# A two-layer block of phase mixer and ternary feed-forward: the context's inverse deviation goes through a DRAM row, and its statistics follow the first hidden unit

## The chip, the cores and the metric

One Trainium2 chip, one of its cores. The metric is the device time of the kernel in microseconds (us), lower is better. Before the change the median of 3 runs is 1516.18 us (1516.14 to 1516.83). One further execution was profiled.

## The reference, cut to what matters

x is 16 sequences of 1024 rows of 256 float32. One layer of each kind is applied:

```python
# mixer, on xn = layernorm(x), with a residual from xn and one from x
omega = xn @ W_omega.T + b_omega
phi = cumsum(omega * exp(log_scale) / sqrt(position), axis=1)
cm_real, cm_imag = xn * cos(phi), xn * sin(phi)
mem_real, mem_imag = cumsum(cm_real) / position, cumsum(cm_imag) / position
ret_real = mem_real * cos(phi) + mem_imag * sin(phi)
ret_imag = mem_imag * cos(phi) - mem_real * sin(phi)
context = concatenate([cm_real, cm_imag, ret_real, ret_imag])      # 1024 wide
h = layernorm(context) * ln_gamma + ln_beta
h = gelu(h @ W1.T + b1)                                            # 512 hidden units
x = x + xn + (h @ W2.T + b2)
# feed-forward with weights quantized to -1, 0, 1, on layernorm(x)
x = x + relu(layernorm(x) @ Wq1.T + b1f) @ Wq2.T + b2f             # 1024 hidden units
```

## The kernel before

The rows are cut into 32 chunks of 512 rows (`CH`), two per sequence. A chunk lives on chip with its features on the 128 partitions and its 512 rows along the free dimension. Matmuls run in float16 with high and low parts (`hi`, `lo`) of activations and weights, so a hidden unit block of the mixer (`hidden`, L967 to L984) takes 24 matmuls of 512 columns.

The kernel is written as one program per engine, each a fixed list of work, tied together by semaphores (`need`, `need_sum`, `need_block` wait for the counter of a named step and chunk). `run` calls `step(s)` for s = -1 to 31 on each engine. In step s, four chunks are in hand: `now` = s (its feed-forward), `nxt` = s+1 (its mixer's two products), `ahead` = s+2 (phases, sums and context), `far` = s+3 (first normalization and the product with W_omega). The order inside a step is written by hand for each engine. Three special stretches stand apart from the 29 full steps (s = 0 to 28): the preparation of weights with step -1, then step 29 which has no `far`, and the last two steps (`last_mixer` and the end of the feed-forward).

TensorE in a full step: `hidden` 0 and 1, `context_stats`, `hidden` 2, `spread`, `hidden` 3, then the feed-forward in a skewed order: `ffn_in` 0 to 3, `ffn_out` 0, `ffn_in` 4, `ffn_out` 1, `ffn_in` 5, `omega`, `ffn_out` 2, `ffn_in` 6, `ffn_out` 3, `ffn_in` 7, `ffn_out` 4, `mixer_out`, `ffn_out` 5 to 7.

The context's layer normalization is folded behind the W1 product. `context_stats` (L952, L958) sums the context and its squares over the features by matmuls with a column of ones, so mean and square sum come out with rows on partitions. `context_variance` on VectorE (L1363 to L1375) makes the variance, `inverse_std_context` on GpSimd (L514) raises it to the power -1/2, into `crs` (128 x 4). But the product with W1 has features on partitions and rows along the free dimension, so the 512 inverse deviations are needed as one row repeated on all 128 partitions (`rb`). `spread` (L965) makes it by four TensorE transposes of a broadcast column of `crs` into PSUM, and `spread_out` on ScalarE (L675) copies it to `rb`. `scale_hidden` on VectorE (L1382) multiplies each of the four hidden blocks in PSUM by `rb`; ScalarE then applies `gelu` (L679) and makes the high part (`gelu_hi`, L685), VectorE the low part (`gelu_lo`, L1387), and `mixer_out` (L1038) reads both.

The feed-forward's hidden block m goes `ffn_in` (L1004) on TensorE, `relu` (L713) and `relu_hi` (L722) on ScalarE, `relu_lo` (L1426) on VectorE, `ffn_out` (L1017) on TensorE. Its input is turned from rows to features by DMA transposes that SyncE issues (L445), after `second_hi` (L695, ScalarE) and `second_lo` (L1418, VectorE).

GpSimd also issues the accumulating DMAs: `base_bias` (L497), `x1_bias` (L501), `output_sum` (L505), `retrieve` (L490, L493) and `square_sums` (L543).

The ternary feed-forward weights are made on chip too: `signs` on VectorE (L1576, L1577) compares with thresholds, `turn_signs` on TensorE (L1134, L1135) turns groups of them, `group_hi` on ScalarE (L849) copies them out.

Of the kernel before, what the change touches and what calls it, by code (L numbers as in the profile page):

```python
# [43 lines left out]
def phase_mixer_layer(nc, x, w_omega, b_omega, log_scale, ln_gamma, ln_beta, w1, b1, w2, b2,  # L44
# [14 lines left out]
    out_v = out.rearrange("b (c t p) d -> (b c) p t d", t=NT, p=P)  # L59

    ctx = ExitStack()
    with ctx:
# [105 lines left out]
        ident_h = rows2[:, 0, 0, 0:P]  # L168
        minus_ident_h = rows2[:, 0, 0, P:2 * P]
# [103 lines left out]
        spread_done, rbs_done = sem("spread_done"), sem("rbs_done")  # L273
# [18 lines left out]
        out_done = sem("out_done")  # L292

# [180 lines left out]
        def _(pool):  # L474
# [65 lines left out]
            def square_sums(c):  # L540
                need(pool, sqr_done, c)
# [6 lines left out]
            def square_lo(c, after):  # L548
                if after:
                    need(pool, frac_done, after)  # L550
# [26 lines left out]
        def _(act):  # L577
# [146 lines left out]
            def last_mixer(before, now, last):  # L724
# [5 lines left out]
                spread_out(last)  # L730
# [15 lines left out]
            def step(s):  # L746
# [24 lines left out]
                if now and now.index == 0:  # L771
                    for n in SIGN_GROUPS[4:6]:
                        group_hi(n)
# [4 lines left out]
                if now and now.index == 0:  # L778
                    for n in SIGN_GROUPS[6:]:
                        group_hi(n)  # L780
# [5 lines left out]
                if now:  # L786
                    second_hi(now)
                if far:
                    normalise_1(far)
                if ahead:  # L790
                    modulated_hi(ahead)
                if far:
                    first_rows_hi(far)
                if nxt:
                    spread_out(nxt)
                    gelu(nxt, 0)
                    gelu(nxt, 1)
                    gelu(nxt, 2)
                    gelu_hi(nxt, 0)
# [11 lines left out]
                if now:  # L811
                    relu(now, 1)
                    relu_hi(now, 1)
# [104 lines left out]
        def _(pe):  # L918
# [9 lines left out]
            def omega(c):  # L928
# [3 lines left out]
                else:  # L932
                    need_turned1(pe, c.index)
                    need(pe, rbs_done, c, 2)
# [782 lines left out]
```

## Time and profile before

| | |
|---|---|
| median of 3 runs | 1516.18 us |
| the profiled execution, its own time | 1516.45 us |
| its span in the profile | 1514.6 us |
| TensorE busy | 1469.5 us, 97% |
| VectorE busy | 1407.4 us, 93% |
| ScalarE busy | 1255.5 us, 83% |
| GpSimd busy | 558.6 us, 37% |
| a full step | 44.85 us |

Busy time is the union of an engine's instructions; an engine that is nearly always busy sets the pace only if the chain of waits runs through it. A full step repeats itself so closely that one of them (that of s = 15, from 780.12 us) can stand for all.

### The profile page before, as it was taken

The page shows a single profiled execution, that of the slowest core. Times are in us where ns is not written, and L with a number is a line of the kernel's source. Part 1 is how long each engine was busy: PE and PEld are TensorE (multiplying, and loading weights), DVE is VectorE, ACT ScalarE, POOL GpSimd, SP SyncE. Part 2 cuts the span into 40 slices and gives each one's busy share as a digit, 9 for nine tenths or more (in the row PEclk, how much of TensorE's full clock was granted, in tenths as well). Part 3 has the DMA queues.
Part 4 walks back from the last instruction along what each step waited for, and adds up shares of the span by engine and source line. Part 5 has one row for each costly group of instructions (what it writes and reads, how often), then busy time and mean ns, then how long its engine had stood idle before and what let it go on. Part 6 is the DMA issues. An engine that isn't in the chain of part 4 may idle for free.

```text
span 1514.6 us, 29961 instructions
## 1 busy us (share of the span) xinstructions
PE 1469.5 (97%) x10685; PEld 880.5 (58%) x10685; DVE 1407.4 (93%) x2325; ACT 1255.5 (83%) x1773; POOL 558.6 (37%) x393
## 2 busy tenths in 40 slices
PE   4789999999999999999999999999999999999998
PEld 3446556656555665656665655666655566565566
DVE  6999999999999999999999999999999999999844
ACT  6769888888888888888888888888888888888756
POOL 1233444432444433344433344444234443334321
PEclk9899999999999999999999999999999999999999
DMA  6445656655756665665665675666576566566542
GB/s 222 78 87 115 124 92 121 126 118 118 139 104 103 123 119 120 132 120 92 125 125 115 123 136 96 111 126 119 115 137 114 96 126 118 120 126 116 91 87 43
DMA packets 236035, 174.98 MB, mean 116 GB/s; under 512 B 139120, under 2 KB 222064, under 8 KB 235888
## 3 DMA queue, kind: packets, MB, share of 16 engines
q0 software_dynamic: 63984, 100.15, 40.5%
q1 hardware_dynamic: 170272, 69.25, 18.8%
q10 hardware_dynamic: 1632, 3.67, 0.7%
q8 instruction: 86, 1.41, 0.4%
q14 instruction: 61, 0.50, 0.1%
HBM read 24.13 MB, written 33.03 MB: 38 GB/s over the span
## 4 chain that ended last, share of the span: by engine, by line
PE 90%; DVE 4%; ACT 2%; issue 2%; DMA 1%; SPq 0%; POOL 0%; DVEq 0%; ACTq 0%; POOLq 0%
PE ps L983 41%; PE ps L1017 15%; PE ps L1004 14%; PE ps L1038 11%; PE ps L939 5%; PE ps L952 3%; DMA ri<-qb 1%; PE ps L965 1%; PE ps L958 0%; DVE ph L1263 0%; SPq L445 0%; DMA lscale<-in_L_attn_log_scale 0%; DVE mr L1311 0%; DVE mi L1297 0%; ACT xs L610 0%
## 5 line engine op out<-in xcount | busy, mean ns | idle before, releaser
L983 PE MATMUL ps<-arena,w_hi 128*128 128x512 f16 x2048 | 609.0, 379 | 0.6 <-DVE arena L1358 0.6
L983 PE MATMUL ps<-arena,w_lo 128*128 128x512 f16 x1024 | 388.1, 379 | 0.0
L983 PEld LDWEIGHTS ps<-arena,w_hi 128*128 128x128 f16 x2048 | 197.8, 98 | 221.8 <-issue 2.0
L1017 PE MATMUL ps<-fw_t,arena 128*128 128x256 f16 x2048 | 254.8, 272 | 1.9 <-DVE arena L1426 1.9
L1004 PE MATMUL ps<-turned,fw_t 128*128 128x512 f16 x1024 | 247.1, 379 | 0.6 <-issue 0.4
L1017 PEld LDWEIGHTS ps<-fw_t,arena 128*128 128x128 f16 x2048 | 195.7, 97 | 69.1 <-issue 30.1
L713 ACT ACTIVATE arena<-ps,relu_bias,relu_scale 128x512 f32<-128x512 f32 x256 | 197.0, 769 | 24.3 <-PE ps L1004 24.0
L1426 DVE TENSOR_TENSOR arena<-arena 128x512 f16<-128x512 f32 x256 | 172.5, 683 | 40.6 <-ACT arena L722 37.2
L1038 PE MATMUL ps<-w_hi,arena 128*128 128x256 f16 x1024 | 174.5, 274 | 4.8 <-DVE arena L1387 4.5
L983 PEld LDWEIGHTS ps<-arena,w_lo 128*128 128x128 f16 x1024 | 100.1, 98 | 120.8
L722 ACT CAST arena<-arena 128x512 f16<-128x512 f32 x256 | 154.5, 615 | 4.3
L1004 PEld LDWEIGHTS ps<-turned,fw_t 128*128 128x128 f16 x1024 | 100.1, 98 | 94.4 <-DMA turned<-rows 0.7
L1038 PE MATMUL ps<-w_lo,arena 128*128 128x256 f16 x512 | 140.4, 274 | 0.0
L546 POOL TENSOR_TENSOR sqr<-sqr 128x512 f32<-128x512 f32 x32 | 48.9, 1528 | 178.0 <-DVE arena L1358 126.5
L490 POOL DMA_DIRECT2D rr<-qa x32 | 29.6, 925 | 225.1 <-DVE rr L1348 225.1
L1038 PEld LDWEIGHTS ps<-w_hi,arena 128*128 128x128 f16 x1024 | 100.7, 98 | 17.6 <-issue 5.4
L560 POOL TENSOR_TENSOR qa<-mi,sn 128x1024 f32<-128x1024 f32 x31 | 73.2, 2362 | 86.4 <-DVE mr L1311 86.4
L610 ACT ACTIVATE xs<-x,lean,rs 128x256 f32<-128x256 f32 x128 | 66.4, 589 | 46.3 <-DVE lean L1212 46.3
L679 ACT ACTIVATE arena<-arena,b_full,z_down 128x512 f32<-128x512 f32 x128 | 96.9, 804 | 1.7 <-DVE arena L1382 1.3
L1382 DVE TENSOR_TENSOR arena<-ps,rb 128x512 f32<-128x512 f32 x128 | 82.0, 682 | 16.4 <-ACT rb L675 12.3
L1387 DVE SCALAR_TENSOR_TENSOR arena<-arena,up 128x512 f16<-128x512 f32 x128 | 92.1, 741 | 0.0
L685 ACT ACTIVATE arena<-arena,up 128x512 f16<-128x512 f32 x128 | 88.1, 713 | 1.1
(189 smaller groups left out, 2745.1 us busy)
## 6 DMA issues: line engine op xcount, KB each, us to landing
x_rows<-in_L_attn_x SPq DMA_DIRECT2D x32, 512.0 KB, 4.7
rr<-qa POOLq DMA_DIRECT2D x32, 512.0 KB, 7.9
ri<-qb POOLq DMA_DIRECT2D x32, 512.0 KB, 8.4
sqr<-turn POOLq DMA_DIRECT2D x32, 512.0 KB, 5.6
base<-bias_rows POOLq DMA_DIRECT2D x32, 512.0 KB, 5.5
x<-bias_rows POOLq DMA_DIRECT2D x32, 512.0 KB, 5.7
out<-x SPq DMA_DIRECT2D x31, 512.0 KB, 5.7
out<-x POOLq DMA_DIRECT2D x31, 512.0 KB, 6.3
```

The lines of the kernel that those rows point to most:

```text
L679: act.activation(z[:, m], z[:, m], ACT.Gelu, scale=z_down[:, 0:1], bias=b1_full[:, m:m + 1])\
L685: act.activation(gh[:, m], z[:, m], ACT.Copy, scale=up[:, 3:4]).then_inc(gh_done[m], 1)
L713: act.activation(rf[:, m % SLOTS], ps[:, 4 + m % KE], ACT.Relu, scale=relu_scale[:, 0:1], bias=relu_bias[:, m:m + 1]).then_inc(relu_done, 1)
L722: act.copy(rh[:, m % SLOTS], rf[:, m % SLOTS]).then_inc(rh_done, 1)
L939: last = pe.matmul(ps[:, 2 + e], w[:, k, e * P:(e + 1) * P], a[:, k], start=(i == 0), stop=(i == len(passes) - 1))
L983: last = pe.matmul(ps[:, 4 + m], w[:, k, m * P:(m + 1) * P], a[:, c.b, k], start=(i == 0), stop=(i == len(passes) - 1))
L1004: last = pe.matmul(ps[:, 4 + m % KE], fw1_t[:, k, m * P:(m + 1) * P], a[:, k], start=(i == 0), stop=(i == len(passes) - 1))
L1017: last = pe.matmul(ps_rows_a[:, j], a[:, m % SLOTS, j * P:(j + 1) * P], fw2_t[:, m], start=(m == 0 and j % 2 == 0 and a is rh), stop=(m == ...
L1038: last = pe.matmul(rows[:, j], a[:, m, j * P:(j + 1) * P], w[:, m], start=(i == 0), stop=(i == len(passes) - 1))
L1382: dve.tensor_tensor(z[:, m], ps[:, 4 + m], rb[:, :], ALU.mult).then_inc(z_done[m], 1)
L1387: dve.scalar_tensor_tensor(out=gl[:, m], in0=z[:, m], scalar=up[:, 3:4], in1=gh[:, m], op0=ALU.mult, op1=ALU.subtract).then_inc(gl_done[m], 1)
L1426: dve.tensor_tensor(rl[:, m % SLOTS], rf[:, m % SLOTS], rh[:, m % SLOTS], ALU.subtract)\
```

## The change

- `spread` and its four transposes leave TensorE, and `spread_out` leaves ScalarE. In their place `deviations_out` issues a DMA from ScalarE's queue that writes `crs` (512 single float32 elements) into a row in DRAM, and `deviations_in` issues another, after the first has landed, that reads the 2 KB row onto all 128 partitions of `rb` (256 KB). `scale_hidden` waits for that.
- `context_stats` follows `hidden` 0 in place of `hidden` 1 (from step 0 on), `context_variance` moves up behind `modulate_imag` on VectorE, `inverse_std_context` moves ahead of `x1_bias` on GpSimd, and `square_lo` goes to the head of GpSimd's step.
- On ScalarE `second_hi` goes ahead of `cosine`, and `relu` 0 with `relu_hi` 0 go ahead of `gelu_hi` 0 and 1, `relu` 1 and `relu_hi` 1 ahead of `gelu_hi` 2. On VectorE `second_lo` moves up (except in step 0), `first_rows_lo` and `memory_real` go ahead of `scale_hidden`, and `relu_lo` 4 ahead of `gelu_lo` 3.
- The second half of the ternary signs moves from step -1 to step 0 on VectorE; their turns and copies move later inside step 0. The thresholds' chain of small operations is moved ahead of `context_lo(first, 3)`.
- `hidden` 0 waits for the four parts of the context one by one instead of all at its start. `omega` and `mixer_out` no longer wait for `rb`.
- In the last step the feed-forward's last two blocks run tile by tile (`last_tiles`), so that `output` can start on half of the rows.

```diff
+    rstd_rows = nc.dram_tensor("rstd_rows", [2, CH], F32).ap()
...
             def inverse_std_context(c):
                 need(pool, cve_done, c)
-                need(pool, spread_done, c, 1)
+                need_sum(pool, row_done, c, 1)
...
-                if nxt and not now:
+                if nxt:
                     square_lo(nxt, ahead)
...
-                if nxt and now:
-                    square_lo(nxt, ahead)
                 if far:
                     inverse_std_1(far)
+                if nxt and now:
+                    inverse_std_context(nxt)
                 if now:
                     x1_bias(now)
-                if nxt:
+                if nxt and not now:
                     inverse_std_context(nxt)
...
-            def spread_out(c):
-                need(act, spread_done, c)
+            def deviations_out(c):
+                need(act, crs_done, c)
+                act.dma_start(rstd_rows[c.b].rearrange("(t p) -> p t", p=P), crs[:, :],
+                              allow_slow_non_contiguous=True).then_inc(row_done, 16)
+
+            def deviations_in(c):
+                need_sum(act, row_done, c)
                 need(act, z_done[KE - 1], c, 1)
-                act.copy(rb[:, :], ps[:, 2]).then_inc(rbs_done, 1)
+                act.dma_start(rb[:, :], rstd_rows[c.b].partition_broadcast(P)).then_inc(rbs_done, 16)
...
                 if now:
                     normalise_2(now)
+                if now and now.index > 0:
+                    second_hi(now)
                 if ahead:
                     cosine(ahead)
...
-                if now:
+                if now and now.index == 0:
                     second_hi(now)
+                if nxt:
+                    deviations_out(nxt)
                 if far:
                     normalise_1(far)
                 if ahead:
                     modulated_hi(ahead)
+                if nxt:
+                    deviations_in(nxt)
                 if far:
                     first_rows_hi(far)
...
                 if nxt:
-                    spread_out(nxt)
                     gelu(nxt, 0)
                     gelu(nxt, 1)
                     gelu(nxt, 2)
...
+                if now:
+                    relu(now, 0)
+                    relu_hi(now, 0)
+                if nxt:
                     gelu_hi(nxt, 0)
                     gelu_hi(nxt, 1)
                 if now:
-                    relu(now, 0)
-                    relu_hi(now, 0)
+                    relu(now, 1)
+                    relu_hi(now, 1)
                 if nxt:
                     gelu_hi(nxt, 2)
...
                 if now:
-                    relu(now, 1)
-                    relu_hi(now, 1)
                     relu(now, 2)
...
-            def spread(c):
-                need(pe, crs_done, c)
-                for j in range(NT):
-                    last = pe.transpose(ps[:, 2, j * P:(j + 1) * P], crs[:, j:j + 1].to_broadcast([P, P]), ident[:, :])
-                last.then_inc(spread_done, 1)
-
...
-                if m == 0:
-                    for part in range(4):
-                        need(pe, ch_done[part], c)
-                        need(pe, cl_done[part], c)
                 for i, (w, a, k) in enumerate(passes):
+                    if m == 0 and i % (3 * KD) == 0:
+                        need(pe, ch_done[k // KD], c)
+                        need(pe, cl_done[k // KD], c)
...
+            def last_tiles(c):
+
+                for m in range(KF - 2, KF):
+                    need_block(pe, rh_done, m, c)
+                    need_block(pe, rl_done, m, c)
+                for j in range(NT):
+                    for m in range(KF - 2, KF):
+                        last = ffn_tile(m, j)
+                    last.then_inc(tile_done, 1)
...
+                    if now:
+                        context_stats(nxt, ahead)
                     hidden(nxt, 1)
...
-                    context_stats(nxt, ahead)
+                    if not now:
+                        context_stats(nxt, ahead)
...
-                    spread(nxt)
...
+                if now and now.index == 0:
+                    dve.wait_ge(p_fw2, 16)
+                    dve.wait_ge(p_tern, 2)
+                    signs(1, fw2_in, fw2_signs)
                 if ahead:
                     modulate_imag(ahead)
+                if nxt and now:
+                    context_variance(nxt)
+                if ahead:
                     sums_imag(ahead)
                 if far:
                     gains_1(far)
+                if now and now.index > 0:
+                    second_lo(now)
...
+                if far:
+                    first_rows_lo(far)
+                if ahead:
+                    memory_real(ahead)
                 if nxt:
                     scale_hidden(nxt, 0)
                     scale_hidden(nxt, 1)
                     scale_hidden(nxt, 2)
-                if far:
-                    first_rows_lo(far)
-                if ahead:
-                    memory_real(ahead)
+                if ahead:
                     retrieve_imag_cos(ahead)
...
```

## Rows read from the trace of the kernel before

**Rows 1.** The page: the chain that ended last, share of the span by engine.
```profile
PE 90%; DVE 4%; ACT 2%; issue 2%; DMA 1%; SPq 0%; POOL 0%; DVEq 0%; ACTq 0%; POOLq 0%
```

**Rows 2.** Windows, one full step: length; busy PE, PEld, DVE, ACT, POOL; clock; DMA.
```profile
780.12:824.97 44.85, 44.85 (x330) 26.77 (x328) 43.27 (x70) 38.31 (x55) 17.61 (x12) 1.00 0.63 118
```

**Rows 3.** Chain of waits through the step from 780.12: start, length, what.
```profile
780.12 10.36 PE ps L983 x48
790.48 1.58 PE ps L952 x64
...
797.46 0.44 PE ps L965 x4
...
803.08 3.45 PE ps L1004 x16
...
808.27 0.98 PE ps L1017 x8
...
816.18 0.93 PE ps L1017 x8
```

**Rows 4.** Timeline of ScalarE in that step: start, length, line, operation, idle before.
```profile
801.97 1.32 ACT L685 ACTIVATE arena<-arena,up 128x512 f16<-128x512 f32 x2
803.98 0.78 ACT L713 ACTIVATE arena<-ps,relu_bias,relu_scale 128x512 f32<-128x512 f32 x1 [0.69 <-PE ps L1004]
804.79 0.62 ACT L722 CAST arena<-arena 128x512 f16<-128x512 f32 x1
805.32 0.72 ACT L685 ACTIVATE arena<-arena,up 128x512 f16<-128x512 f32 x1
805.94 0.76 ACT L713 ACTIVATE arena<-ps,relu_bias,relu_scale 128x512 f32<-128x512 f32 x1
806.73 0.62 ACT L722 CAST arena<-arena 128x512 f16<-128x512 f32 x1
```

**Rows 5.** Timeline of VectorE in the same step.
```profile
798.61 1.89 DVE L1382 TENSOR_TENSOR arena<-ps,rb 128x512 f32<-128x512 f32 x3 [0.19 <-ACT rb L675]
...
807.38 0.69 DVE L1426 TENSOR_TENSOR arena<-arena 128x512 f16<-128x512 f32 x1
```

**Rows 6.** Chain of waits, step 29: a late low part, and TensorE behind it.
```profile
1439.52 0.14 issue
1439.65 1.03 PE ps L1017 x8
...
1441.55 0.87 PE ps L1017 x8
```

**Rows 7.** DMA issues of the whole span: count, KB each, median us to landing.
```profile
base<-bias_rows POOLq DMA_DIRECT2D x32, 512.0 KB, 5.5
...
out<-x SPq DMA_DIRECT2D x2, 256.0 KB, 2.2
...
b_raw<-in_L_attn_b SPq DMA_DIRECT2D x1, 2.0 KB, 8.9
fb<-in_L_ffn_b SPq DMA_DIRECT2D x1, 4.0 KB, 14.5
```

**Rows 8.** Timeline of the start, all engines: step -1 and step 0.
```profile
78.07 2.08 ACT L600 ACTIVATE qb<-x_rows,lean,rs 128x256 f32<-128x256 f32 x4 [1.21 <-issue]
...
80.01 1.92 POOL L514 TENSOR_TENSOR crs<-cve,minus_half 128x4 f32<-128x4 f32 x1 [4.84 <-DVE cve L1375]
...
94.81 1.27 DVE L1576 TENSOR_SCALAR arena<-arena,thr 128x2048 f16<-128x2048 f32 x1
...
103.61 1.23 DVE L1358 TENSOR_TENSOR arena<-ri,arena 128x1024 f16<-128x1024 f32 x1 [1.79 <-ACT arena L642]
...
130.15 1.04 PE L1004 MATMUL ps<-turned,fw_t 128*128 128x512 f16 x4 [0.26 <-DMA turned<-rows]
```

**Rows 9.** Chain of waits through the end of step 30.
```profile
1474.97 3.45 PE ps L1004 x16
...
1478.71 5.41 PE ps L1038 x48
```

More of the change, by code:

```diff
@@ L549, in square_lo @@
                 if after:
-                    need(pool, frac_done, after)
+                    need(pool, y_done, after)
                 need(pool, q_done, c)
@@ L729, in last_mixer @@
                 second_hi(now)
-                spread_out(last)
+                deviations_out(last)
+                deviations_in(last)
                 for m in range(KE - 1):
@@ L798, in step @@
                     gelu(nxt, 2)
+                if now and now.index == 0:
+                    for n in SIGN_GROUPS[6:]:
+                        group_hi(n)
+                if now:
+                    relu(now, 0)
+                    relu_hi(now, 0)
+                if nxt:
                     gelu_hi(nxt, 0)
@@ L1015, in ffn_out, with ffn_tile @@
                 for j in range(NT):
[L1016 to L1019 removed]
+                    last = ffn_tile(m, j)
                 last.then_inc(f2_done, 1)
+            def ffn_tile(m, j):
+                for a in (rh, rl):
+                    last = pe.matmul(ps_rows_a[:, j], a[:, m % SLOTS, j * P:(j + 1) * P], fw2_t[:, m],
+                                     start=(m == 0 and j % 2 == 0 and a is rh), stop=(m == KF - 1 and a is rl),
+                                     skip_group_check=True)
+                return last
+            def last_tiles(c):
[4 more added lines that the diff above has]
+                    for m in range(KF - 2, KF):
+                        last = ffn_tile(m, j)
+                    last.then_inc(tile_done, 1)
             def mixer_out(c, before):
@@ L1072, in step @@
                             turn_signs(n)
-                    spread(nxt)
+                    if now and now.index == 0:
+                        for n in SIGN_GROUPS[4:6]:
+                            turn_signs(n)
                     hidden(nxt, 3)
+                    if now and now.index == 0:
+                        for n in SIGN_GROUPS[6:]:
+                            turn_signs(n)
                     if not now:
@@ L1087, in step @@
                             ffn_out(now, m - LAG)
-                    for m in range(KF - LAG, KF):
+                    for m in range(KF - LAG, KF if nxt else KF - 2):
                         ffn_out(now, m)
@@ L1091, in step @@
                             last_transposes(nxt)
+                    if not nxt:
+                        last_tiles(now)
                     return
@@ L1483, in step @@
                     carry_imag(ahead)
-                if nxt:
+                if nxt and not now:
                     context_variance(nxt)
-                if now:
+                if now and now.index == 0:
                     second_lo(now)
@@ L1533, in step @@
                     gelu_lo(nxt, 2)
-                    gelu_lo(nxt, 3)
                 if now:
                     relu_lo(now, 4)
+                if nxt and now:
+                    gelu_lo(nxt, 3)
                 if ahead:
@@ L1666, in _ @@
             context_lo(first, 2, rr[:, :, :])
-            context_lo(first, 3, ri[:, :, :])
-            phase_turns(second)
-            phase_sums(second)
-            carry_phase(second)
             dve.wait_ge(p_spread, 3)
@@ L1685, in _ @@
             dve.tensor_scalar(thr[:, :], thr[:, :], 0.5, None, ALU.mult).then_inc(p_thr, 1)
+            context_lo(first, 3, ri[:, :, :])
+            phase_turns(second)
+            phase_sums(second)
+            carry_phase(second)
             prepared(dve)
```

41 lines of the change are left out of this document (14 added, 27 removed).

## The prediction

> **What bounds the kernel now.** I read the chain that ended last first. It lies on TensorE for 90% of the span [rows 1], so VectorE's and ScalarE's high busy shares do not set the pace. Then the window of one full step, cut from the start of one `hidden` 0 to the next: TensorE is busy for all of 44.85 us, at the full clock [rows 2]. VectorE has 1.6 us of room and ScalarE 6.5. Then the chain inside that step, in order of time [rows 3]: every piece is a TensorE piece. The four turns of `spread` are one of them, 0.44 us. Two pieces of `ffn_out` are longer than the rest. A block of 8 matmuls takes 0.87 us where nothing holds it [rows 6]; `ffn_out` 1 takes 0.98 and `ffn_out` 4 takes 0.93 [rows 3]. So 0.17 us of the step are small waits for the low parts, and a TensorE that never waits would take 44.68 us. The reader is to see two things: TensorE can only gain what is taken from its own list, and `ffn_out` 1 already starts on the last moment.
>
> **Turns removed.** TensorE loses 0.44 us a step [rows 3]. Its pure list is then 44.68 - 0.44 = 44.24 us. If nothing waits, the 29 full steps give 29 x 0.61 = 17.7 us.
>
> **What ScalarE's new order costs.** The chain from the end of `ffn_in` 0 to `ffn_out` 1 can be read off the timeline. `ffn_in` 0 is the first of the four in the 3.45 us piece at 803.08, so it ends at 803.08 + 0.86 = 803.94. `relu` 0 starts 0.04 later, at 803.98, after 0.69 us of idle time; `relu_hi` 0 at 804.79; one `gelu_hi` (block 2) at 805.32; `relu` 1 at 805.94; `relu_hi` 1 at 806.73, done 0.62 later [rows 4]. `relu_lo` 1 runs on VectorE from 807.38 for 0.69 us [rows 5]. TensorE needs another 0.14 us after such an end [rows 6]. That is 0.04 + 0.81 + 0.53 + 0.62 + 0.79 + 0.65 + 0.69 + 0.14 = 4.27 us. TensorE's own work between the two, three `ffn_in`, `ffn_out` 0 and `ffn_in` 4, is 808.27 - 803.94 = 4.33 us. The two match, which is why 0.11 us shows there.
>
> In the new order `gelu_hi` 0 and 1 no longer run in ScalarE's idle time ahead of `relu` 0; they stand between `relu_hi` 0 and `relu` 1, where one `gelu_hi` stood. Two of them take 0.60 + 0.62 = 1.22 us start to start (the merged pair shows 1.32 with the tail of the second [rows 4]) in place of 0.62. The chain becomes 4.27 + 0.60 = 4.87 us, TensorE's work stays 4.33, and `ffn_out` 1 waits 0.54 us. A block of `ffn_out` whose low part came late also took 1.03 us in place of 0.87, 0.16 more [rows 6], since its weights could not be loaded ahead. `relu_lo` 4, moved ahead of `gelu_lo` 3, is early, so the 0.06 there goes. The step becomes 44.24 + 0.54 + 0.16 = 44.94 us against 44.85: the 0.44 is given back. Over 29 steps that is +2.6 us. Bounds: 29 x -0.61 = -17.7 (the low parts do not bind), and +0.25 a step or +7 if `ffn_out` 3, which has 0.15 us of room by the same sums, waits too.
>
> **The DRAM row: is it hidden?** Positions are us after the step's start. `context_stats` ends at 5.2 + 1.8 = 7.0 (half the 10.36 piece, then L952 and L958 [rows 3]). VectorE, busy with `modulate_imag` until 7.5, finishes the variance at 8.1. GpSimd's power takes 1.92 [rows 8] after `inverse_std_1`, which I place at 6.6 to 8.5, so `crs` is there at 10.5. ScalarE issues the write at about 10.7, behind `cosine`. No row has a write of 512 single elements. The nearest are the two loads of single elements queued on one another: 2.31 + 14.5 = 16.8 for 1024 elements, and 1.76 + 8.9 = 10.7 for 512, so 1024 cost 6.1 and 512 about 3.1 us under a loaded start [rows 7]; with a landing of some 2.2 us, that of the 256 KB store at the idle end [rows 7], an estimate of 5.3, bounds 2.2 and 8.9. The row is in DRAM at 16.0. `deviations_in` is queued behind `normalise_1` and `modulated_hi`, which end at 15.2, so ScalarE stands 0.8 us, and `first_rows_hi` and VectorE's `first_rows_lo` behind it are later by as much. The read is 256 KB: 2.2 in the quiet, 5.5 for the 512 KB that GpSimd's queue moves in this stretch [rows 7]; I take 3.5 with the issue, so `rb` is there at 19.5 to 20. VectorE gets to `scale_hidden` 0 at 20.2 anyway, its three blocks take 1.9 [rows 5], the three `gelu` behind them end at about 23.1. `relu` 0 cannot start before `ffn_in` 0 has ended, at 22.5 + 0.86 + 0.04 = 23.4 in the shorter list. So I cost the DRAM row at nothing, with 0.3 us of cover left. Gone that cover, each further us delays `relu` 0 and with it `ffn_out` 1: 1 us a step, 29 us in all.
>
> By the Trainium skill (DMA: Bandwidth & Descriptors, Anatomy of one DMA) a DMA costs about 2.0 us plus bytes/436e3; as an estimate by that page the 256 KB read takes 2.6, which the 2.2 of the idle store [rows 7] agrees with, and the same page (Specifications) has transfers under 512 B done by read-modify-write, which speaks against the 4-byte writes and which no row here shows. By the page's 2.6 `rb` comes 0.9 us earlier than in my sum and the row stays hidden.
>
> **Moves that I cost at nothing.** `square_lo` at the head of GpSimd's step pushes `base_bias` and `inverse_std_2` back by at most 0.7 us; `lean_2` on VectorE asks for the latter only at 6.3, when it is there (5.9). The new wait of `inverse_std_context` is for the row of the chunk before, a step old; `x1_bias`, behind it, is 1 us later, and its readers a dozen. `second_lo` is done some 2.5 us earlier, and with it the transposes for `ffn_in` 0, which cover their sharing with the two new DMAs. VectorE takes its blocks in another order, and `scale_hidden` 3 is done at 23.4, before `ffn_in` 3 asks for it at 25.1; all of it fits in the idle time before `relu_lo` 0. If that cover failed, up to 0.5 us a step.
>
> **Step -1 and step 0.** In step -1 the power still runs from 80.01 to 81.93 [rows 8], but ScalarE's write now stands in front of `normalise_1`, which started at 78.07 [rows 8]. It would start at about 82.4: +4.3 us for it, `modulated_hi`, `first_rows_hi`, and behind these VectorE's `first_rows_lo`, `scale_hidden`, and the retrieved products. The early thresholds give back 0.35. The DMA of the retrieved imaginary part had VectorE wait 1.8 us before `context_lo` 3 at 103.61 [rows 8]; I take half of the delay, +2.1 us, for VectorE's entry into step 0 (bounds 0 and 4). Then `signs`, two operations of 1.2 us [rows 8], hidden in step -1, are on VectorE ahead of `second_lo` 0: +2.4. Behind it stand the transposes and `ffn_in` 0, which had TensorE waiting at 130.15 already [rows 8]. Small gains there -0.3. Together +4.2 us, bounds 0 and +7.
>
> **The end.** In step 30 the hidden blocks are scaled while `hidden` 3 runs, so `mixer_out` no longer waits: it started at 1478.71, 0.3 us after `ffn_in` 3 ended at 1474.97 + 3.45 [rows 9], and 0.44 goes with the turns: -0.7. Step 29, without `omega`, gets +0.2. The tile order gains about 0.1: the last block's low part arrives when TensorE would be in block 6.
>
> **Sum.** +2.6 + 4.2 + 0.2 - 0.7 - 0.1 = +6.2 us on the profiled 1516.45 (span 1514.6 and 1.85 around it), 1522.65. The median is 0.27 lower, so I say 1522.4 us, 0.4% slower.
>
> **Rivals.**
> A: the low parts do not bind. Then each full step is 44.24 us, -17.7, and with +4.2 and -0.6 of the ends the time is 1516.2 - 14.1 = 1502 us. For it: the turns leave the busiest engine. Against it: six start times of ScalarE in sequence, which leave no slack.
> B: the row comes late. The write shares the DMA engines with `output_sum`, `x1_bias` and the feed-forward's transposes. It decides once write and read together take over 9.1 us, against my 8.8. With 1.5 us more, 29 x 1.2 = +35: 1557 us. For it: the 8.9 us landing of 512 elements [rows 7], and cover of only 0.3 us. Against it: that landing stood behind two larger loads on its queue.
> A rule that would bring B about stands in the Trainium skill (Perfetto Trace Analysis, DMA Instruction — HWDGE): one descriptor generator is locked for a DMA's issue, so ScalarE's read would wait for SyncE's transposes; no row here shows ScalarE issuing beside a transpose.
> C: the exchange is even. The start costs 0 instead of 4.2 (ScalarE's wait in step -1 is covered by the DMA that is waited for there): 1516.2 + 6.2 - 4.2 = 1518.2 us.
>
> **Chances.** My forecast 0.36, A 0.22, B 0.24, C 0.18. Under 0.2% (3 us) a measurement of this kernel can hardly be told from no change. A is faster, with 0.02 of C; the rest of C within 0.2%, with 0.04 of my forecast's low end; the rest slower: 0.24, 0.20, 0.56. The likeliest case alone spans 1518 to 1528. The range takes in A's end, where the ends cost nothing less, and most of B: 1500 to 1550 us.
>
> **What the profile would show.** L965 gone; a full step of 44.9 us; in the chain, `ffn_out` 1 behind VectorE's L1426 in each step, TensorE idle 0.5 us there, and ScalarE idle ahead of `relu` 0 behind TensorE, not behind the read of `rb`. `ffn_in` 0 of step 0 at about 134 us, behind the transposes. I am wrong if the step is 44.3 (A), if ScalarE or VectorE wait for the DMA of `rb` and the step is over 45.5 (B), or if step 0 comes no later than before (C).

## The result, and the profile after

The changed kernel takes 1659.95 us, median of 4 runs (1658.24 to 1662.16), against 1516.44 us for the kernel before in the same comparison: the ratio is 1.0946, 95% interval 1.0932 to 1.096. It is 9.5% slower. I had said 1522.4 us, in a range of 1500 to 1550.

The page of the changed kernel: busy time of each engine, then the chain that ended last by engine.

```profile
PE 1500.6 (90%) x10557; PEld 874.0 (53%) x10557; DVE 1383.4 (83%) x2325; ACT 1244.3 (75%) x1741; POOL 540.4 (33%) x393
...
DVE 26%; DMA 24%; ACT 22%; issue 15%; PE 11%; ACTq 0%; POOL 0%; SPq 0%; DVEq 0%
```

TensorE held 90% of the chain before [rows 1]; now it holds 11%, and the DMAs 24%. One full step, from `hidden` 0 at 809.15 to the next, in the windows view (length; busy PE, PEld, DVE, ACT, POOL; granted clock; DMA):

```profile
809.15:858.40 49.25, 46.10 (x327) 26.76 (x325) 42.91 (x73) 37.86 (x54) 17.07 (x12) 0.97 0.72 113
```

The step was 44.85 us and all TensorE [rows 2]. The mean of the last 27 full steps is 49.19. Counted from the first matmul of `hidden` 0 in each step, the 28 full steps behind step 0 make 120.6 of the 144.3 us by which the span grew. The start, with step 0 in it, has 18.0, step 29 has 1.5 and the end 4.1. The chain of waits in that step, in order of time:

```profile
820.36 0.46 ACT cs L642
820.82 7.97 DMA rstd_rows<-crs
828.80 3.88 DMA rb<-rstd_rows
832.68 1.47 issue
834.15 0.70 DVE arena L1411
```

The write and the read are both on the path, 13.3 us from the write's issue to the first `scale_hidden` (L1411). The 1.47 us listed as issue belong to the read as well: `scale_hidden` waits for nothing else there, and 3.88 + 1.47 = 5.35 us agrees with the read's median landing of 5.2 us. ScalarE's timeline shows who stands behind the write:

```profile
828.80 0.34 ACTq L685 DMA_DIRECT2D rb<-rstd_rows  x1
829.24 1.05 ACT L700 CAST xs<-qb 128x1024 f16<-128x1024 f32 x1 [3.65 <-DMA rstd_rows<-crs]
```

`deviations_in` (L685) waits in ScalarE's order for the write, and `first_rows_hi` (L700) 3.65 us behind it. On VectorE `first_rows_lo` (L1269) waits for that, and the scaling for the read:

```profile
830.32 1.23 DVE L1269 TENSOR_TENSOR xs<-qb,xs 128x1024 f16<-128x1024 f32 x1 [2.76 <-ACT xs L700]
831.46 1.22 DVE L1354 TENSOR_TENSOR mr<-mr,pos_inv 128x1024 f32<-128x1024 f32 x1
834.15 1.89 DVE L1411 TENSOR_TENSOR arena<-ps,rb 128x512 f32<-128x512 f32 x3 [1.47 <-issue]
```

`ffn_in` 0 waits for the scaling: it writes into the PSUM bank that `scale_hidden` 0 reads. TensorE's timeline here, then the same 16 matmuls in the kernel before, then `ffn_in`'s group over the whole changed kernel, and the granted clock (the third number from the end) of that stretch in windows:

```profile
834.99 5.30 PE L1014 MATMUL ps<-turned,fw_t 128*128 128x512 f16 x16 [3.15 <-DVE arena L1411]
```

```profile
802.92 3.62 PE L1004 MATMUL ps<-turned,fw_t 128*128 128x512 f16 x16
```

```profile
L1014 PE MATMUL ps<-turned,fw_t 128*128 128x512 f16 x1024 | 287.8, 424 | 85.3 <-DVE arena L1411 80.0 <-DMA turned<-rows 4.0 <-issue 0.4
```

```profile
835.00:840.20 5.20, 5.20 (x17) 2.05 (x18) 4.51 (x6) 5.17 (x8) 0.00 (x0) 0.67 0.44 109
836.00:837.00 1.00, 1.00 (x4) 0.30 (x2) 1.00 (x2) 1.00 (x2) 0.00 (x0) 0.50 0.32 64
```

TensorE was idle for 3.15 us; from about 0.8 us after it has begun again the granted clock is 0.50, the lower level of 1.2 GHz, for about 3.4 us. The four `ffn_in` take 5.30 us in place of 3.62. For TensorE these terms close the step: 44.85 - 0.44 (turns) + 3.15 (idle) + 1.68 (clock) = 49.24, against 49.25. Over the whole kernel `ffn_in` is busy for 287.8 us in place of 247.1, so the clock has 1.4 us of a mean step. This is TensorE's own account only. The chain that ended last runs over VectorE, ScalarE and the two DMAs; the write alone is 16% of it and the read 7%.

DMA issues (name, queue, count, KB each, median us to landing) and queues (packets, MB, share of 16 engines) of the changed kernel:

```profile
q0 software_dynamic: 63984, 100.15, 47.5%
...
q10 hardware_dynamic: 23136, 12.13, 3.7%
...
rb<-rstd_rows ACTq DMA_DIRECT2D x32, 256.0 KB, 5.2
...
turned<-rows SPq DMA_TRANSPOSE x124, 6.9
turned<-xs SPq DMA_TRANSPOSE x120, 2.5
...
rstd_rows<-crs ACTq DMA_DIRECT2D x32, 2.0 KB, 8.1
```

The transposes in the kernel before:

```profile
turned<-rows SPq DMA_TRANSPOSE x124, 2.5
```

The write of 2 KB takes 8.1 us. Those that run beside it are slow too: `turned<-rows`, the transposes for `ffn_in`, take 6.9 us in place of 2.5, while `turned<-xs`, at another place of the step, stays at 2.5. A small part of this comes with the moves alone: with the turns back (e1_turns_back, below) `turned<-rows` takes 3.2.

The start and the end, from the chain of waits (the first two lines: step -1 and step 0; the last two: step 30):

```profile
80.85 9.92 DMA rstd_rows<-crs
...
131.20 8.23 DMA rstd_rows<-crs
...
1601.14 9.00 DMA rstd_rows<-crs
1610.16 4.07 DMA rb<-rstd_rows
```

### The profile page after: what moved, and what is told of

Same layout as the page of the kernel before. It is cut to its first block, busy times and chain, and to the rows that moved or that the text cites. A ratio compares the mean times of both kernels' runs of the same rounds, so it can differ in the third digit from the quotient of the medians.

```text
span 1658.9 us, 29736 instructions
## 1 busy us (share of the span) xinstructions
PE 1500.6 (90%) x10557; PEld 874.0 (53%) x10557; DVE 1383.4 (83%) x2325; ACT 1244.3 (75%) x1741; POOL 540.4 (33%) x393
## 3 DMA queue, kind: packets, MB, share of 16 engines
q0 software_dynamic: 63984, 100.15, 47.5%
q10 hardware_dynamic: 23136, 12.13, 3.7%
## 4 chain that ended last, share of the span: by engine, by line
DVE 26%; DMA 24%; ACT 22%; issue 15%; PE 11%; ACTq 0%; POOL 0%; SPq 0%; DVEq 0%
DMA rstd_rows<-crs 16%; DMA rb<-rstd_rows 7%; ACT arena L723 6%; DVE arena L1387 5%; DVE ph L1292 4%; ACT arena L689 4%; PE ps L1014 4%; ACT xs L615 3%; ACT arena L695 3%; PE ps L1063 3%; DVE bn L1225 3%; DVE bn L1430 3%; DVE arena L1455 2%; PE ps L1033 2%; DVE x L1423 2%
## 5 line engine op out<-in xcount | busy, mean ns | idle before, releaser
L1014 PE MATMUL ps<-turned,fw_t 128*128 128x512 f16 x1024 | 287.8, 424 | 85.3 <-DVE arena L1411 80.0
L1014 PEld LDWEIGHTS ps<-turned,fw_t 128*128 128x128 f16 x1024 | 106.3, 107 | 217.8 <-DMA turned<-rows 94.3
L1411 DVE TENSOR_TENSOR arena<-ps,rb 128x512 f32<-128x512 f32 x128 | 82.2, 684 | 56.9 <-issue 38.2
L1269 DVE TENSOR_TENSOR xs<-qb,xs 128x1024 f16<-128x1024 f32 x30 | 36.8, 1228 | 103.9 <-ACT xs L700 103.9
L700 ACT CAST xs<-qb 128x1024 f16<-128x1024 f32 x30 | 31.4, 1047 | 122.6 <-DMA rstd_rows<-crs 122.6
```

Of the source, the lines that this page charges most:

```text
L1014: last = pe.matmul(ps[:, 4 + m % KE], fw1_t[:, k, m * P:(m + 1) * P], a[:, k], start=(i == 0), stop=(i == len(passes) - 1))
L1411: dve.tensor_tensor(z[:, m], ps[:, 4 + m], rb[:, :], ALU.mult).then_inc(z_done[m], 1)
```

## The experiments

Two theories of the 144 us. **The row**: write and read do not fit ahead of `scale_hidden`, and the small pieces slow what runs beside them. **The orders**: the new orders on VectorE and ScalarE cost by themselves. All times are medians; ratios are to the kernel before, with 95% intervals; "step" is the mean full step.

**Turns back (e1_turns_back).** The changed kernel with TensorE's turns and ScalarE's copy again, all else as changed.

```diff
-                    deviations_out(nxt)
...
-                    deviations_in(nxt)
                 if far:
                     first_rows_hi(far)
+                if nxt:
+                    spread_out(nxt)
...
                     hidden(nxt, 2)
+                    spread(nxt)
```

> The changed kernel with the four turns and ScalarE's copy put back where they were in the kernel before, every other part of the change kept. Theory R (the DRAM row is the whole loss in a full step): the 3 us of waiting ahead of ffn_in 0 and the long ffn_in blocks go. If my sum for ScalarE's new order holds as well (ffn_out 1 waits 0.54 + 0.16 us), a full step is 44.68 + 0.7 = 45.4 us and the time about 1516 + 29 x 0.53 + 3 = 1535 us. Rival O (the order costs nothing): step 44.7 to 44.9 us, time 1513 to 1522 us. Rival T (the reordered rest is itself at fault for the loss): over 1600 us.

1568.03 us, ratio 1.0341 (1.0326 to 1.0357), step 46.40. This lies in none of the ranges that I expected (1535; 1513 to 1522; over 1600). The row beside these orders is worth 92 us, and 52 us remain without it, where I had some 19. A sign of them is on VectorE and GpSimd, in the timelines of this kernel:

```profile
826.34 1.22 DVE L1269 TENSOR_TENSOR xs<-qb,xs 128x1024 f16<-128x1024 f32 x1
...
827.48 3.37 DVE L1354 TENSOR_TENSOR mr<-mr,pos_inv 128x1024 f32<-128x1024 f32 x1
```

```profile
826.41 3.35 POOL L564 TENSOR_TENSOR qa<-mi,sn 128x1024 f32<-128x1024 f32 x1 [5.32 <-DVE mr L1340]
```

`memory_real` (L1354) takes 3.37 us and GpSimd's product (L564) 3.35. In the kernel before they took 1.21 and 2.36, the product beside `scale_hidden`:

```profile
798.40 2.36 POOL L560 TENSOR_TENSOR qa<-mi,sn 128x1024 f32<-128x1024 f32 x1 [2.84 <-DVE mr L1311]
...
801.76 1.21 DVE L1325 TENSOR_TENSOR mr<-mr,pos_inv 128x1024 f32<-128x1024 f32 x1
```

**The row alone (e2_row_alone).** The kernel before, with `spread` and `spread_out` replaced by the two DMAs and no order changed (the write ahead of `first_rows_hi`, the read behind it).

```diff
                 if nxt:
+                    deviations_out(nxt)
+                if far:
+                    first_rows_hi(far)
+                if nxt:
+                    deviations_in(nxt)
-                    spread_out(nxt)
...
-                    spread(nxt)
```

> The kernel before with the DRAM row alone in place of the turns; statistics still follow hidden 1, all orders as before. Theory R: the power ends 15.4 us into the step, the write lands 8 us later, the read 5 us after that, so scale_hidden starts near 29 to 30 in place of 18.5, and TensorE, which asks at 22.4, waits about 8 us: step 52 to 54 us, time 1750 to 1790 us. Rival (the loss comes from how the row meets the moved transposes and x1_bias, not from its length): step under 50 us, time under 1660 us.

1855.94 us, ratio 1.2242 (1.2224 to 1.2261), step about 55.4. Its waits (engine, line, waited for: us, times, longest):

```profile
DVE arena L1383 <- DMA rb<-rstd_rows: 371.0, 31, 15.0
```

It is more than I expected (52 to 54 us a step, 1750 to 1790 us). TensorE's wait of 8.4 us (median) is near my 8, but the write took 10.1 us where I had 8, and the lower clock behind the wait was in no term: `ffn_in` is busy for 316.2 us in place of 247.1, 2.2 us a step. The 196 us between this kernel and the changed one are what the other moves of the change do for the row.

**16-byte pieces (e3_16_bytes).** Each partition writes its four values as one run; the read stays contiguous and `scale_hidden` reads `rb` with a stride of four elements instead.

```diff
-                act.dma_start(rstd_rows[c.b].rearrange("(t p) -> p t", p=P), crs[:, :],
-                              allow_slow_non_contiguous=True).then_inc(row_done, 16)
+                act.dma_start(rstd_rows[c.b].rearrange("(p t) -> p t", t=NT), crs[:, :]).then_inc(row_done, 16)
```

> The changed kernel, but the row is written in the order of the partitions: 128 pieces of 16 bytes in place of 512 of 4, and scale_hidden reads rb with a stride of 16 bytes. Theory N (the write's 8 us is the number of its pieces): it lands in 3 to 4.5 us, rb is there 3.5 to 5 us earlier, the step falls from 49.2 to 45 to 46.5 us, time 1530 to 1580 us. Rival Q (its 8 us is queueing among the 512 KB accumulating DMAs of GpSimd's queue): it still lands in 7 us or more and the time stays above 1640 us. Half of each would give about 1610 us. If strided reads of rb are slow on VectorE, L1411 or its successor goes from 0.68 us to above 1 us.

1597.99 us, ratio 1.054 (1.0524 to 1.0556), step 47.35. Landing of the write, then queues and groups of this kernel (the groups: busy us, mean ns):

```profile
DMA to landing us min/median/max: 1.4/1.8/3.6
```

```profile
q0 software_dynamic: 63984, 100.15, 39.6%
...
q10 hardware_dynamic: 10848, 12.13, 2.8%
...
turned<-rows SPq DMA_TRANSPOSE x124, 4.1
```

```profile
L1411 DVE TENSOR_TENSOR arena<-ps,rb 128x512 f32<-128x512 f32 x128 | 131.0, 1062 | 12.9 <-DMA rb<-rstd_rows 8.8 <-PE ps L992 4.1
...
L1353 DVE TENSOR_TENSOR mr<-mr,pos_inv 128x1024 f32<-128x1024 f32 x32 | 101.4, 3170 | 0.0
```

The same 2 KB lands in 1.8 us in place of 8.1, sooner than the 3 to 4.5 that I expected, and 62 us are back; the time is still above the 1530 to 1580 that I had. Number and size of the pieces change together here, so the run does not tell one from the other. The packets fall by 23136 - 10848 = 12288, 384 for each of 32 writes: 128 pieces in place of 512. GpSimd's DMAs, whose bytes are the same, take 39.6% in place of 47.5% of the engines' time. By the Trainium skill (DMA: Bandwidth & Descriptors, Rules for kernel authors) an access that is not contiguous in its last dimension becomes one descriptor per element and should be rearranged; the packet counts agree. What this kernel still lacks lies on VectorE: the strided scaling takes 1062 ns in place of 684 (4 x 0.38 = 1.5 us a step), and with `rb` early `memory_real` meets GpSimd's product again (3170 ns in the mean; in the changed kernel the late row had kept them apart, 1.22 us).

**The read waits for nothing (e4_row_before).** The read takes the row that the chunk before wrote, so the deviations of another chunk are applied; write and read are as many and as large, but overlap.

```diff
+                first = isinstance(c.index, int) and c.index == 0
-                need_sum(act, row_done, c)
+                need_sum(act, row_done, c, 0 if first else 1)
...
-                act.dma_start(rb[:, :], rstd_rows[c.b].partition_broadcast(P)).then_inc(rbs_done, 16)
+                act.dma_start(rb[:, :], rstd_rows[c.b if first else 1 - c.b].partition_broadcast(P))\
+                   .then_inc(rbs_done, 16)
```

> The changed kernel, but from the second chunk on the read takes the row of the chunk before, which has long landed, so nothing waits for the write, while both DMAs still run; the deviations applied are those of another chunk. Theory R with the read alone: rb is there 16 + 5 = 21 us into the step, 0.5 us past the cover; step 45.0 to 45.8 us, time 1525 to 1550 us. Rival D (the write slows the transposes that feed ffn_in 0, which land no earlier than rb did): ScalarE no longer waits but TensorE still stands ahead of ffn_in 0 for the transposes, step 47.5 to 49 us, time above 1600 us.

1600.94 us, ratio 1.0558 (1.0541 to 1.0576), step 47.36. The theory of the read alone (1525 to 1550 us) is wrong, the rival right in its place and, barely, in its time (above 1600 us). The wait for the write is worth 59 us. The other 33 above the turns come though nobody waits for the write: the read takes 8.5 us beside it, `turned<-rows` 7.5, and TensorE now waits for those:

```profile
PE ps L1016 <- DMA turned<-rows: 47.4, 25, 5.5
```

**The orders taken back on the turns (e5_scale_first, e6_both_orders).** First VectorE's, then ScalarE's as well.

```diff
-                if far:
-                    first_rows_lo(far)
-                if ahead:
-                    memory_real(ahead)
                 if nxt:
                     scale_hidden(nxt, 0)
                     scale_hidden(nxt, 1)
                     scale_hidden(nxt, 2)
+                if far:
+                    first_rows_lo(far)
                 if ahead:
+                    memory_real(ahead)
                     retrieve_imag_cos(ahead)
...
+                if nxt:
+                    gelu_hi(nxt, 0)
+                    gelu_hi(nxt, 1)
                 if now:
                     relu(now, 0)
                     relu_hi(now, 0)
                 if nxt:
-                    gelu_hi(nxt, 0)
-                    gelu_hi(nxt, 1)
+                    gelu_hi(nxt, 2)
                 if now:
                     relu(now, 1)
                     relu_hi(now, 1)
-                if nxt:
-                    gelu_hi(nxt, 2)
```

> The kernel with the turns back (the run of the turns put back), and on VectorE scale_hidden 0 to 2 again ahead of first_rows_lo and memory_real, as before the change. Theory P: GpSimd's product runs beside these operations; the multiply of mr with the table reads two operands from SBUF and stands for 2.15 us until GpSimd's is done (3.37 us in place of 1.21 in that run), while scale_hidden reads one of its two from PSUM and does not. Then L1354 is back at 1.2 us, the step falls from 46.3 to my 45.4 us, time 1535 to 1545 us. Rival (the 1.5 us of a step come from something else that moved): time within 5 us of 1568.

> The same with ScalarE's gelu_hi 0 and 1 also again ahead of relu 0 as before. My sum for the chain from ffn_in 0 to ffn_out 1 (4.87 against 4.27 us) gives 0.6 us a step: step 44.7 to 44.9 us, time 1517 to 1526 us, of which 8 us or less are the start of the kernel. Rival (that chain does not bind once scale_hidden is early): no difference to the run without this edit.

1536.39 us, ratio 1.0126 (1.0111 to 1.0141), step 45.41; then 1518.47, ratio 1.0008 (0.9998 to 1.0017), step 44.81. Both are as expected. So of the 52 us VectorE's order has 32 and ScalarE's 18. All other moves together (statistics after `hidden` 0, `second_lo` early, `square_lo`, signs in step 0, `last_tiles`), in a kernel that keeps the turns, end within 2 us of the kernel before: in the profiled executions `hidden` 0 of step 1 starts 1.9 us later, and the 28 steps behind it win back 1.2.

**Each order alone on the kernel before (e8_gelu_hi_late, e9_scale_late).** The same two edits the other way round, one at a time.

> The kernel before with ScalarE's new order alone (relu 0 and relu_hi 0 ahead of gelu_hi 0 and 1, relu 1 and relu_hi 1 ahead of gelu_hi 2). My sum of the prediction taken alone: ffn_out 1 waits 0.6 us more in each of 29 steps, step 45.4 us, time 1531 to 1536 us. Rival (no effect): 1515 to 1518 us.

> The kernel before with VectorE's new order alone (first_rows_lo and memory_real ahead of scale_hidden 0 to 2). Theory P: memory_real stands behind GpSimd's product, scale_hidden 0 starts at 22.9 in place of 18.5 us into the step, and relu 0 behind gelu and gelu_hi 3 us later; step 47 to 48 us, time 1580 to 1610 us. Without that conflict (rival: 1.2 us for memory_real) scale_hidden starts at 20.7 and the step is at most 45.5 us, time below 1536 us.

ScalarE's: 1535.98 us, ratio 1.0124 (1.0109 to 1.0139), step 45.47, as expected. The chain of waits of that kernel, from `ffn_in` 0 to `ffn_out` 1:

```profile
813.37 0.88 PE ps L1006 x4
...
815.61 1.33 ACT arena L685 x2
816.94 0.68 ACT arena L713
...
817.64 0.63 ACT arena L722
...
818.29 0.70 DVE arena L1428
818.99 0.14 issue
819.13 1.03 PE ps L1019 x8
```

From 814.25, the end of `ffn_in` 0, to 819.13 it is 4.88 us, where I had 4.87, and the late block takes 1.03.

VectorE's: 1600.83 us, ratio 1.0549 (1.0532 to 1.0567), step 47.65:

```profile
797.68 3.44 POOL L560 TENSOR_TENSOR qa<-mi,sn 128x1024 f32<-128x1024 f32 x1 [2.72 <-DVE mr L1311]
...
798.83 3.37 DVE L1325 TENSOR_TENSOR mr<-mr,pos_inv 128x1024 f32<-128x1024 f32 x1
802.12 1.87 DVE L1382 TENSOR_TENSOR arena<-ps,rb 128x512 f32<-128x512 f32 x3
```

In this kernel the step begins at 779.27, so `scale_hidden` 0 starts 22.9 us into it; before it was 18.65, counted in the same way (from 779.96, the first matmul of `hidden` 0, to 798.61 [rows 5]). The 4.2 us are 2.3 for the two operations ahead of it and 2.15 for a wait inside `memory_real`, less 0.2 by which they begin earlier. Time and step are as expected. The lines of e1_turns_back show its form. The product starts at 826.41, while `first_rows_lo` runs until 827.56; 2.2 us behind that, at 829.76, the product ends; `memory_real` ends at 830.85, 1.1 us behind the product. The three go one after the other: the product stands behind `first_rows_lo`, `memory_real` behind the product. In the kernel before `scale_hidden`, with one operand in PSUM, ran beside the product: 1.89 us for three [rows 5] and 2.36. By the Trainium skill (SBUF — State Buffer, SBUF: two separate sides) a VectorE operation with two SBUF inputs and a GpSimd operation that reads SBUF exclude each other, each for its whole instruction; these lines agree.

**The row with the old orders (e11_row_good_orders).** The changed kernel with both edits of e6_both_orders.

> Edit: the changed kernel, 4-byte row and no turns, with the old orders of VectorE (scales ahead of first_rows_lo and memory_real) and ScalarE (gelu_hi 0 and 1 ahead of relu 0). It isolates the row beside the 1518 us of the kernel with turns and the same orders. Theory (the row's landing sets the scales, at 25 us after the step's start, some 5 us after VectorE could start them; and what stands behind them on VectorE is late as well): the step is 49 us or more and the time 1640 to 1700 us, so the row costs 120 to 180 us against these orders, and the changed kernel's late scales had hidden a part of the wait. Rival (row and orders are independent costs that add): 1660 less the 50 us that the orders cost beside the turns, about 1610 us, step 47.7.

The four executions took 1687.08, 1708.82, 1713.39 and 3888.9 us, so no ratio is given; what held the last one up, nothing here shows. The profiled one is that of 1708.82, step 50.81. Of the three that lie near each other one is inside my 1640 to 1700 and two are above it; the rival's 1610 is far off. VectorE in it:

```profile
853.87 1.89 DVE L1411 TENSOR_TENSOR arena<-ps,rb 128x512 f32<-128x512 f32 x3 [6.74 <-DMA rb<-rstd_rows]
```

The costs do not add. With turns the new orders cost 50 us (1518 to 1568). With the row they save 27 to 53, by the three executions of 1687 to 1713 against 1660: `scale_hidden` 0 starts as late in both kernels (24.6 and 24.7 us into the step, medians), but `first_rows_lo` and `memory_real` now stand behind it, where in the changed kernel they fill a part of VectorE's wait. The row costs 169 to 195 us with the old orders and 92 with the new.

**Can the row be hidden at all (e7_16_bytes_orders, e10_copied, e12_read_early)?** e7: 16-byte pieces, VectorE's old order, and ScalarE's `gelu_hi` 0 ahead of `relu` 1, 1 and 2 behind it. e10: besides, the DMA fills `rb_raw`, and one ScalarE copy puts it in row order, so that VectorE reads `rb` contiguously. e12: besides, the read is issued ahead of `modulated_hi`, a `gelu` of one column draws the load of the function table into the wait, and the signs are back in step -1.

```diff
+                act.copy(rb[:, :].rearrange("q (t p) -> q t p", p=P),
+                         rb_raw[:, :].rearrange("q (p t) -> q t p", t=NT)).then_inc(rbs_done, 1)
...
+                if nxt:
+                    deviations_in(nxt)
                 if ahead:
                     modulated_hi(ahead)
-                if nxt:
-                    deviations_in(nxt)
```

> The 16 byte variant of the DRAM row (no turns), with scale_hidden 0 to 2 ahead of first_rows_lo and memory_real again, and on ScalarE relu 0, relu_hi 0, gelu_hi 0, relu 1, relu_hi 1, gelu_hi 1 and 2. rb is there 19 us into the step, in time. TensorE's list is 44.24 us; against it stand VectorE's scale_hidden at 1.06 us in place of 0.68 (1.5 us a step, in 1.6 us of room). If that fits, step 44.4 to 44.9 us and time 1506 to 1525 us, the first version that uses the gain; if VectorE becomes the bound, step 45.3 to 46 us and time 1535 to 1555 us.

> Edit: the kernel with 16-byte pieces and the good orders, and the strided reading of rb leaves VectorE: the DMA fills a raw buffer, ScalarE copies it once a step into rb in row order (128x512, some 0.9 to 1.1 us by VectorE's strided scale of 1086 ns), and the three-or-four scales run at the contiguous 684 ns. Theory (with short pieces gone, what is left of the 36 us is VectorE's strided reading, 4 x 0.4 = 1.6 us a step on an engine that had become the bound): VectorE gets back 1.6 us a step, the step falls from 45.94 to 44.4 to 44.9, time 1506 to 1525 us, L1411-like lines near 0.68 us. Rival (the bound is the arrival of rb, at some 18.2 us after the step's start plus now 1 us of copy): VectorE waits for rb as before, scales end no earlier, the step stays at 45.3 or over and the time at 1535 or over.

> Edit: the kernel with 16-byte pieces, good orders and ScalarE's copy, and three things more. deviations_in goes ahead of modulated_hi, so the read is issued about 0.9 us earlier (at 1222.4 in place of 1223.26 in the step where the copy started at 1228.67); an idle gelu of one column ahead of the copy draws the 1.28 us load of the function table into the wait for the read; the second half of the signs goes back to step -1 (VectorE's 2.4 us). Theory (every late step of that kernel is late by the arrival of rb): the mean full step falls from about 45.65 by 0.6 to 0.9 to 44.75 to 45.05, and with 1 to 2 us of the start the time is 1518 to 1530 us: about the kernel before, since VectorE waits for rb still in the steps that carry the phase. Rival (the read is slowed by what it shares the DMA engines with, so that an earlier issue lands no earlier; or VectorE is the bound): mean step 45.4 or more, time 1538 us or over.

1552.8 us (ratio 1.0231, 1.0214 to 1.0248; step 45.94), 1546.84 (1.0186, 1.0161 to 1.021; step 45.67) and 1540.08 (1.0145, 1.0114 to 1.0177; step 45.50). e7 lies in the range that I gave for VectorE as the bound, but e10 speaks against that reading; in both e10 and e12 the rival was right. In e10 VectorE gets its 1.5 us a step back and waits for the copy instead, 77.9 us in all. The read of e10, then of e12, to its landing:

```profile
rb_raw<-rstd_rows ACTq DMA_DIRECT2D x32, 256.0 KB, 4.5
```

```profile
rb_raw<-rstd_rows ACTq DMA_DIRECT2D x32, 256.0 KB, 5.4
```

Issued 0.9 us earlier in the mean, it took about 0.9 longer and landed 0.2 earlier. In e10 steps of 44.5 to 45.0 us (44.55 in most, 0.30 shorter than those of the kernel before) alternate with steps of 45.4 to 50.5. In every one of the longer ones VectorE's copy of the phase carry (128x2) takes 1.16 us, and the read lands at 19.1 to 21.0 us after the step's start in place of 17.6 to 18.6. The copy in the kernel before, then in e10:

```profile
L1270 DVE COPY ph_carry<-ph 128x2 f32<-128x2 f32 x16 | 2.8, 176 | 1.6
```

```profile
L1307 DVE COPY ph_carry<-ph 128x2 f32<-128x2 f32 x16 | 17.6, 1098 | 1.6
```

It takes 0.2 us in the kernel before and in e2, e8 and e9, where `square_lo` is at its old place, and 1.1 in every kernel profiled here that has `square_lo` at the head of GpSimd's step. There the two run at the same time, in the changed kernel's step from 810.58 and 810.61, 1.16 us each. Nothing that was run moves `square_lo` alone, so that it makes the longer steps is likely and not shown. So where the row is in time, 0.30 of the turns' 0.44 us are gained. But no kernel tried here beats the kernel before; e6_both_orders, which keeps the turns, equals it.

## Why the prediction was wrong

- **The step that failed: "So I cost the DRAM row at nothing, with 0.3 us of cover left."** I had the write issued at 10.7 us after the step's start, landed at 16.0, and `rb` at 19.5 to 20. It was 11.7, 19.7 and 25.0 in the step shown, and 11.1, 19.5 and 24.6 in the mean of 28 steps. The write took 8.1 us, where I took 5.3 and had 8.9 as a bound; the read 5.2, where I took 3.5. Their sum of 13.3 stands against the threshold of 9.1 that I gave. The estimate of 2.6 us for the read beside my sum is refuted as well: the quickest of the 32 took 3.3.
- **The price was right by luck.** My price for each us beyond the threshold gives 29 x 4.2 = 122 us, near the 120.6 measured. But by my own places the threshold is 9.8 (`scale_hidden` at 20.2, with 0.3 of cover, against a write issued at 10.7), not 9.1, and would give 29 x 3.5 = 102. The path was another one too: I had the late row delay `relu` 0 and `ffn_out` 1, and left out that `ffn_in` 0 waits for `scale_hidden` 0. There TensorE stood for 3.15 us in the step shown. And about 1.4 us of a step are TensorE's lower clock, which was in no term of mine.
- **Where the size came from.** I divided a landing of 1024 single elements by two. Those were loads; the nearest row for a slow DMA under load was the upper bound, 8.9, and with 0.3 us of cover the middle was no safe choice. I treated the small pieces as slow for themselves only. They slow what runs beside them: the transposes take 6.9 us, with 16-byte pieces 4.1 (e3) and with no row 3.2 (e1), and the read takes 8.5 us where it runs beside the write (e4).
- **Moves costed at nothing.** I wrote that VectorE's order "fits in the idle time before `relu_lo` 0" and that without the cover it was up to 0.5 us a step. Alone it costs 2.8 us a step (e9_scale_late), on the turns 1.0 (e1 to e5). I had not looked at what GpSimd runs beside the moved `memory_real`. In the changed kernel itself this cost does not show: the row is later still. `square_lo`, also costed at nothing beyond its own 0.7 us, now runs beside VectorE's copy of the phase carry, which takes 1.1 us in place of 0.2. In the changed kernel the write is issued at 11.6 to 11.9 us in 13 of the 14 full steps with that copy and at 10.3 to 10.9 in the others.
- **ScalarE's new order.** The chain of 4.87 us was measured as 4.88, and by this order alone the step rose by 0.62, where my terms give 0.59: 0.54 + 0.16, less the 0.11 that `ffn_out` 1 had waited already. This step of the prediction was right, and hidden in the changed kernel by a larger wait.
- **Start and end.** I had +4.2 for the start; up to step 1 it is 18.0, of which some 4 are step 0's share as a full step. The write took 9.9 us in step -1 and 8.2 in step 0, and both stand in the chain (I had the wait for it at nothing in both). With turns and old orders the start is +1.9, so the signs cost less than the 2.4 I gave them. Step 29 and the end together were to gain 0.6 and lost 5.6: with write and read at 9.0 and 4.1 us, `mixer_out` waits for the `gelu`s.
- **The rivals.** B was right in its mechanism: the row comes late and is waited for. Its threshold was not put to a test, since 13.3 lies far beyond it; its time of 1557 us took 1.5 us more than my 8.8 as the size, where it was 4.5. The lock of the descriptor generator which I put beside it did not bring it about: ScalarE's read issue took 0.34 to 0.36 us in each full step, and in the step shown it stood (828.80 to 829.14) inside one of SyncE's transpose issues (827.90 to 829.44). The clause "I am wrong if ... VectorE wait for the DMA of `rb` and the step is over 45.5" is what happened. A and C had the row hidden.

## What to carry to other kernels

A DMA in place of on-chip work is free only while issue, landing and whatever waits in the same in-order queue fit ahead of the consumer. Write the threshold down, and if the bound of an unmeasured landing lies beyond it, as here, give the late case a larger chance than the 0.24 it had. Write a small tile with each partition's values in one run, not element by element. Before moving a VectorE operation with two SBUF operands, look at what GpSimd runs at its new place. Judge orders and the wait they were made for together: here the same orders cost 50 us without the late row and saved 27 to 53 with it.

## What the runs showed of the hardware

- 512 pieces of 4 bytes to DRAM land in 8.1 us (median; 10.1 in e2), 128 pieces of 16 bytes in 1.8, the 2 KB being the same. The transposes beside them take 6.9 us, 4.1 with the 16-byte pieces, and 3.2 with no row (e1).
- A VectorE product of two SBUF operands and a GpSimd product at the same time did not overlap: 3.37 and 3.35 us in place of 1.21 and 2.36, each with its wait for the other engine in it.
- A VectorE copy of 128x2 float32 took 1.10 us in place of 0.18 in the kernels where a GpSimd subtraction of 128x512 ran at the same time.
- VectorE's 128x512 float32 product read an operand with a stride of four elements in 1062 ns in place of 684 (e3).
- TensorE, idle for 3.15 us, had the lower clock for about 3.4 of the next 5.3 us, which cost 1.7 us on four blocks of `ffn_in`.
